# Last four stages of a hybrid model in one residency: the stream and its normalised form kept in SBUF from the fourth layer norm to the experts

## The reference, cut to what matters

```python
def _ln_t(v, eps=1e-5):
    m = jnp.mean(v, axis=-1, keepdims=True)
    s = jnp.var(v, axis=-1, keepdims=True)
    return (v - m) / jnp.sqrt(s + eps)
...
t = t + _L3_attn_ref(_ln_t(t), L3_attn_Wk, L3_attn_Wq, L3_attn_Wv)
t = t + _L3_ffn_ref(_ln_t(t), L3_ffn_router_w, L3_ffn_router_b, L3_ffn_expert_w, L3_ffn_expert_b)
```

## Time and profile before

| | before |
|---|---|
| median of three runs | 11067.49 us |
| the profiled execution | 11073.83 us, span 11072.0 us |
| TensorE busy | 10046.5 us, 91% of the span |
| VectorE busy | 6934.8 us, 63% |
| DRAM traffic of the queue of SyncE's DMAs | 1010.30 MB |
| ln4, from its first DMA issue to that of l3 | 10606.62 to 10664.38 us: 57.8 us |
| l3, to the first issue of ln5 | 10664.38 to 10770.31 us: 105.9 us |
| ln5, to the first issue of moe | 10770.31 to 10828.32 us: 58.0 us |
| moe, to the end | 10828.32 to 11072.0 us: 243.7 us |

### The profile page before, as it was taken

The page is one execution under the profiler, slowest core; times in us unless marked ns, Lnnn a source line. Parts: engine busy times, 40 slices in busy tenths (PEclk is TensorE's granted clock), DMA queues, the critical chain, the costliest instruction groups (busy, mean ns, idle before and its releaser), DMA issues. The chain is left out here.

```text
span 11072.0 us, 146129 instructions
## 1 busy us (share of the span) xinstructions
PE 10046.5 (91%) x45360; PEld 7803.1 (70%) x45360; DVE 6934.8 (63%) x8005; ACT 5276.4 (48%) x13704; POOL 5609.9 (51%) x2968
## 2 busy tenths in 40 slices
PE   7999999999967699999999689998599999999977
PEld 5677677667743588888888456565388887888854
DVE  6677677667755699999999644343533333333337
ACT  4787787778743677777777222222111111111110
POOL 4797788779743699999999126463100000000000
PEclk9999999999987799999999789999799999999988
DMA  2111111111124544444444510001745555455521
GB/s 81 26 39 40 38 30 38 41 26 39 32 88 163 189 107 108 105 108 108 105 105 108 195 56 8 14 10 73 254 123 130 128 128 159 127 133 123 125 105 64
DMA packets 646817, 1018.65 MB, mean 92 GB/s; under 512 B 285816, under 2 KB 347776, under 8 KB 631552
## 3 DMA queue, kind: packets, MB, share of 16 engines
q1 hardware_dynamic: 646176, 1010.30, 32.8%
HBM read 717.21 MB, written 211.03 MB: 84 GB/s over the span
## 5 line engine op out<-in xcount | busy, mean ns | idle before, releaser
L687 POOL TENSOR_TENSOR l_probs_low<-l_probs,l_probs_high 128x512 fp32r<-128x512 f32 x1792 | 2385.8, 1361 | 795.3 <-ACT l_probs_high L657 781.6
L1374 POOL TENSOR_TENSOR m_c_h<-m_h,m_c 128x2048 f32<-128x2048 f32 x520 | 2341.9, 4578 | 45.9 <-DVE m_h L1361 45.7
L1361 DVE TENSOR_TENSOR_SCAN m_h<-m_decay,m_ps_x 128x1024 f32<-128x1024 f32 x1040 | 2272.4, 2262 | 92.3 <-issue 64.5
L1274 PE MATMUL m_ps_y<-m_c_h,m_ident 128*128 128x256 f32 x8320 | 1981.6, 381 | 2.2 <-POOL m_c_h L1374 2.2
L743 DVE TENSOR_REDUCE l_max_by_row<-l_ps_all 128x8 f32<-128x512 f32 x2048 | 1358.0, 685 | 524.9 <-PE l_ps_all L506 444.4
L1274 PEld LDWEIGHTS m_ps_y<-m_c_h,m_ident 128*128 128x128 f32 x8320 | 1512.8, 191 | 174.1 <-POOL m_c_h L1374 4.9
L655 ACT ACTIVATE l_probs<-l_ps_all 128x512 f32<-128x512 f32 x2048 | 1240.4, 606 | 452.8 <-PE l_ps_all L547 307.0
L2350 PE MATMUL s_ps_all<-s_toeplitz,s_u_high 128*128 128x512 f32 (+1 forms) x4608 | 1327.9, 372 | 59.4 <-DMA s_toeplitz<-filters 50.3
L657 ACT ACTIVATE l_probs_high<-l_ps_all 128x512 fp32r<-128x512 f32 x2048 | 1233.0, 602 | 0.0
L2404 ACT ACTIVATE s_filtered_high<-s_rows 128x512 fp32r<-128x512 f32 x384 | 242.8, 632 | 1764.3 <-DVE s_rows L2477 898.4
L2350 PEld LDWEIGHTS s_ps_all<-s_toeplitz,s_u_high 128*128 128x128 f32 x4608 | 845.9, 189 | 240.0 <-DMA s_toeplitz<-filters 51.3
(11 more groups left out here) (320 smaller groups left out, 15384.1 us busy)
## 6 DMA issues: line engine op xcount, KB each, us to landing
m_delta_u<-du_t SPq DMA_DIRECT2D x1040, 128.0 KB, 3.7
s_toeplitz_sums<-filters SPq DMA_DIRECT2D x192, 642.0 KB, 6.7
s_toeplitz_sums<-filters SPq DMA_DIRECT2D x192, 386.0 KB, 5.7
m_c<-c_windows SPq DMA_DIRECT2D x130, 512.0 KB, 4.2
s_toeplitz<-filters SPq DMA_DIRECT2D x64, 770.0 KB, 9.3
s_toeplitz<-filters SPq DMA_DIRECT2D x64, 642.0 KB, 10.4
l_q_and_row_bias<-l_q_parts SPq DMA_DIRECT2D x64, 512.0 KB, 5.0
du_t<-m_delta_u_high SPq DMA_DIRECT2D x128, 256.0 KB, 3.1
```

The source lines that it names most:

```text
L687: pool.tensor_tensor(pl[:, slot, :], pt[:, slot, :], f(ph[:, slot, :]), ALU.subtract).then_inc(low_pool, 1)
L1274: ins = pe.matmul(y_ps[:, group % 2, 0:DIRS * SPAN].rearrange("p (d t) -> p d t", d=DIRS), ident[:, :], ch[:, group % CH, :, n, :], start= ...
L1361: dve.tensor_tensor_scan(h[:, u % H, :], decay[:, pair % 2, ct, k % 2, :, :].rearrange("p n t -> p (n t)"), x_ps[:, u % X, :], 0.0, ALU.mu ...
L1374: pool.tensor_tensor(ch[:, group % CH, 2 * pair % DIRS:2 * pair % DIRS + 2, :, :].rearrange("p d n t -> p d (n t)"), h[:, 2 * pair % H:2 * ...
```

## The change

The four stages get one common `Mem` in a new function `tail`. It holds the stream (`xs`), its normalised form (`xc`), and every weight but the experts' bias. `norm_kept` takes the place of `layer_norm`: the same arithmetic in the same order, but it reads the stream from the kept tile and leaves the normalised form in the other kept tile. The first of the two calls also loads the stream and nine weight tensors; the second issues no DMA. Neither stores anything. `linear_attention` and `experts` lose their loads (all but the experts' bias), their waits for them, and `linear_attention` its stores. Each of the four still opens its own `Mem` for its other tiles and semaphores, so the meeting of the engines between stages stays; `tail`'s own `Mem` adds one more closing block, with nothing to clear, at the very end.

```diff
+def norm_kept(nc, stage, xs, xc, cm, ident, eps, x=None, loads=()):
...
+        @block.sync
+        def _(sp):
+            if x is not None:
+                for dst, src in loads[:2]:
+                    sp.dma_start(dst[:], src).then_inc(weights, 16)
+                for q in range(LOTS):
+                    part = slice(q * LOT * TW, (q + 1) * LOT * TW)
+                    sp.dma_start(xs[:, part], x[:, part]).then_inc(loaded[q], 16)
+                for dst, src in loads[2:]:
+                    sp.dma_start(dst[:], src).then_inc(others, 16)
+                sp.wait_ge(others, 16 * (len(loads) - 2))
...
-def linear_attention(nc, stage, xn, x, x_out, wk_t, wq, wv_t, ident_in):
+def linear_attention(nc, stage, xs, res, ident, wks, wqs, wvs):
...
-        @block.sync
-        def _(sp):
-            for dst, src in ((ident, ident_in), (wks, wk_t), (wvs, wv_t), (wqs, wq), (xs, xn), (res, x)):
-                sp.dma_start(dst[:], src).then_inc(loaded, 16)
-            for b in range(BATCH):
-                sp.wait_ge(added, NTB * (b + 1))
-                sp.dma_start(x_out[:, b * L:(b + 1) * L], res[:, b * L:(b + 1) * L]).then_inc(stored, 16)
-            sp.wait_ge(stored, 16 * BATCH)
...
-            pe.wait_ge(loaded, 96)
...
-            dve.wait_ge(loaded, 96)
...
-def experts(nc, stage, xn, x, out, router_w, router_b, expert_w, expert_b, ident_in, rank_in):
+def experts(nc, stage, xs, res, out, ident, rw, rb, ew, rank, expert_b):
...
-            loads = ((ident, ident_in), (rw, router_w), (ew, expert_w), (rb, router_b),
-                     (rank, rank_in), (xs, xn), (res, x))
-            for dst, src in loads:
-                sp.dma_start(dst[:], src).then_inc(loaded, 16)
...
-            pe.wait_ge(loaded, 112)
...
-            dve.wait_ge(loaded, 112)
...
+def tail(nc, stage, x, out, a):
+
+    H, KQ, E = 8, 64, 8
+    with Mem(nc, stage) as keep:
+        xs, xc = keep.sb("x", [P, TOK]), keep.sb("xn", [P, TOK])
...
+        loads = ((cm, a["channel_mean"]), (ident, a["ident"]), (wks, a["wk_t"]), (wvs, a["wv_t"]), (wqs, a["wq_heads"]),
+                 (rw, a["router_w"]), (rb, a["router_b"]), (rank, a["rank8"]), (ew, a["expert_w"]))
+        norm_kept(nc, "ln4", xs, xc, cm, ident, 1e-5, x=x, loads=loads)
+        linear_attention(nc, "l3", xc, xs, ident, wks, wqs, wvs)
+        norm_kept(nc, "ln5", xs, xc, cm, ident, 1e-5)
+        experts(nc, "moe", xc, xs, out, ident, rw, rb, ew, rank, a["expert_b"])
...
-    xn4, x5, xn5 = act_map("xn4"), act_map("x5"), act_map("xn5")
-    layer_norm(nc, "ln4", x4, xn4, a["channel_mean"], a["ident"], 1e-5)
-    linear_attention(nc, "l3", xn4, x4, x5, a["wk_t"], a["wq_heads"], a["wv_t"], a["ident"])
-    layer_norm(nc, "ln5", x5, xn5, a["channel_mean"], a["ident"], 1e-5)
-    experts(nc, "moe", xn5, x5, out, a["router_w"], a["router_b"], a["expert_w"], a["expert_b"], a["ident"], a["rank8"])
+    tail(nc, "tail", x4, out, a)
```

More of the change, by code:

```diff
@@ L2503, in _, with at, take_variance, spread_out @@
             add(PASSES - 1, 7)
-def linear_attention(nc, stage, xn, x, x_out, wk_t, wq, wv_t, ident_in):
+def norm_kept(nc, stage, xs, xc, cm, ident, eps, x=None, loads=()):
+    LOT = 4
+    LOTS, COLS = NT // LOT, LOT * TW // P
+    with Mem(nc, stage) as m:
+        sq = m.sb("square", [P, TOK])
+        epst = m.sb("eps", [P, 1])
+        std, rstd = m.sb("deviation", [P, LOTS, COLS]), m.sb("reciprocal", [P, LOTS, COLS])
+        mean_ps, var_ps, wide_ps = m.ps("mean", [P, 2, TW]), m.ps("variance", [P, 2, TW]), m.ps("reciprocal", [P, 2, TW])
+        weights, own, loaded = m.sem("weights"), m.sem("own"), [m.sem(f"loaded{q}") for q in range(LOTS)]
+        mean, centred, squared, variance, deviation, recip, spread, normed, others = (
+            m.sem(n) for n in ("mean", "centred", "squared", "variance", "deviation", "recip", "spread", "normed", "others"))
+        block = m.block()
+        def at(t):
+            return slice(t * TW, (t + 1) * TW)
+        @block.sync
[9 more added lines that the diff above has]
+                sp.wait_ge(others, 16 * (len(loads) - 2))
+        @block.tensor
+        def _(pe):
+            if x is not None:
+                pe.wait_ge(weights, 32)
+            def take_variance(t):
+                q, k = t // LOT, t % LOT
+                pe.wait_ge(squared, t + 1)
+                if k == 0 and q >= 2:
+                    pe.wait_ge(deviation, q - 1)
+                for n in range(TW // P):
+                    col = k * (TW // P) + n
+                    ins = pe.matmul(var_ps[:, q % 2, col:col + 1], sq[:, t * TW + n * P:t * TW + (n + 1) * P], cm[:, 0:1], start=True, stop=True)
+                ins.then_inc(variance, 1)
+            def spread_out(t):
+                q, k = t // LOT, t % LOT
+                pe.wait_ge(recip, q + 1)
+                if t >= 2:
+                    pe.wait_ge(normed, t - 1)
+                for n in range(TW // P):
+                    col = k * (TW // P) + n
+                    ins = pe.matmul(wide_ps[:, t % 2, n * P:(n + 1) * P], rstd[:, q, col:col + 1].to_broadcast((P, P)), ident[:, :], start=True, stop=True)
+                ins.then_inc(spread, 1)
+            for t in range(NT):
+                if t % LOT == 0 and x is not None:
+                    pe.wait_ge(loaded[t // LOT], 16)
+                if t >= 2:
+                    pe.wait_ge(centred, t - 1)
+                pe.matmul(mean_ps[:, t % 2, :], cm[:, :], xs[:, at(t)], start=True, stop=True).then_inc(mean, 1)
+                if t >= 1:
+                    take_variance(t - 1)
+                if t >= LOT + 2:
+                    spread_out(t - LOT - 2)
+            take_variance(NT - 1)
+            for t in range(NT - LOT - 2, NT):
+                spread_out(t)
+        @block.scalar
+        def _(act):
+            act.wait_ge(own, 1)
+            for t in range(NT):
+                q = t // LOT
+                act.wait_ge(centred, t + 1)
+                act.activation(sq[:, at(t)], xc[:, at(t)], ACT.Square).then_inc(squared, 1)
+                if t % LOT == LOT - 1:
+                    act.wait_ge(variance, t + 1)
+                    act.activation(std[:, q, :], var_ps[:, q % 2, 0:COLS], ACT.Sqrt, bias=epst[:, :]).then_inc(deviation, 1)
+        @block.vector
+        def _(dve):
+            dve.memset(epst[:, :], eps).then_inc(own, 1)
+            def normalise(t):
+                dve.wait_ge(spread, t + 1)
+                dve.tensor_tensor(xc[:, at(t)], xc[:, at(t)], wide_ps[:, t % 2, :], ALU.mult).then_inc(normed, 1)
+            def invert(q):
+                dve.wait_ge(deviation, q + 1)
+                dve.reciprocal(rstd[:, q, :], std[:, q, :]).then_inc(recip, 1)
+            for t in range(NT):
+                dve.wait_ge(mean, t + 1)
+                if t % LOT == 0 and x is not None:
+                    dve.wait_ge(loaded[t // LOT], 16)
+                dve.tensor_tensor(xc[:, at(t)], xs[:, at(t)], mean_ps[:, t % 2, :], ALU.subtract).then_inc(centred, 1)
+                if t % LOT == 1 and t > LOT:
+                    invert(t // LOT - 1)
+                if t >= LOT + 2:
+                    dve.wait_ge(squared, t - LOT - 1)
+                    normalise(t - LOT - 2)
+            invert(LOTS - 1)
+            for t in range(NT - LOT - 2, NT):
+                dve.wait_ge(squared, t + 1)
+                normalise(t)
@@ L2520, in linear_attention @@
         mix_ps = m.ps("mix", [P, TW])
-        loaded, turned, copied, grammed = (m.sem(n) for n in ("loaded", "turned", "copied", "grammed"))
+        turned, copied, grammed = (m.sem(n) for n in ("turned", "copied", "grammed"))
         gram_ok, kg_done, kg_ok, ktv_done, ktv_ok, mixed, mix_ok = (
             m.sem(n) for n in ("gram_ok", "kg_done", "kg_ok", "ktv_done", "ktv_ok", "mixed", "mix_ok"))
-        outed, added, stored = m.sem("outed"), m.sem("added"), m.sem("stored")
+        outed, added = m.sem("outed"), m.sem("added")
         block = m.block()
-        @block.sync
-        def _(sp):
-            for dst, src in ((ident, ident_in), (wks, wk_t), (wvs, wv_t), (wqs, wq), (xs, xn), (res, x)):
-                sp.dma_start(dst[:], src).then_inc(loaded, 16)
-            for b in range(BATCH):
-                sp.wait_ge(added, NTB * (b + 1))
-                sp.dma_start(x_out[:, b * L:(b + 1) * L], res[:, b * L:(b + 1) * L]).then_inc(stored, 16)
-            sp.wait_ge(stored, 16 * BATCH)
         @block.tensor
         def _(pe):
-            pe.wait_ge(loaded, 96)
             for b in range(BATCH):
@@ L2617, in experts @@
         xt_ps = m.ps("x_by_token", [P, 2, TW])
-        loaded, own = m.sem("loaded"), m.sem("own")
+        own = m.sem("own")
         logits, gated, shifted, expd, mixed, turned, accd, turned_ok = (
```

10 lines of the change are left out of this document (4 added, 6 removed).

## The result

Five runs of the changed kernel against five of the kernel before: median 10996.56 us (10976.72 to 11021.98) against 11067.49 us (11065.08 to 11083.72); ratio 0.9934, 95% interval 0.9918 to 0.9950. The forecast was 10989 us, a ratio of 0.9929. The profiled execution took 10996.56 us with a span of 10994.8 us.

A forecast was written before the change was run, and what follows sets the result against it. At three seams, 77.62 us together, DMA alone was on the path; elsewhere the compute engines set the pace. 73.1 + 1.9 + 1.5 + 2.4 - 0.5 = 78.4 us off 11067.5 gave 10989 us, range 10975 to 11003.

The forecast's parts named there:

- three terms of 30.86, 12.25 and 30.01 us: Time removed at seams ln4/l3, l3/ln5 and ln5/moe, leaving 1.5 us at each; together 73.1 us.
- The added loads: Seven more weight loads in ln4, 1.55 MB, 4.5 us of transfer, hidden behind the stream's parts; taken as nothing.
- Rival 3: In ln4 the added weight loads delay the stream by 4.5 us: 73.9 us saved, 10993.6 us; chance 0.05.
- sum of three terms less the closing block: Clock gains at stage starts, 1.9 us in l3, 1.5 in ln5, 2.4 in moe, less 0.5 for tail's closing block.
- an idle time of 2.3 us: TensorE's pause at a seam, claimed just short enough that each following stage starts at 2.4 GHz.
- 2.5 us of logits at double pace: At moe's start the logits run at the full clock for 2.5 us before it falls, winning 2.4 us.
- Rival 1: In moe the logits hold the full clock, winning 13.8 us instead of 2.4: 10977.7 us; chance 0.09.
- Rival 2: Stage starts cost more than 1.5 us and the clock gains are lost: 66.9 us saved, 11000.6 us; chance 0.09.
- rival 5: At the seams another engine is late by as much, so nothing is gained: about 11067 us; chance 0.02.
- rival 4: moe's expert loop slows as VectorE's tiles lie elsewhere; 0.122 us per instruction would cancel the gain; chance 0.01.

The follow-up runs named there:

- e8: Changed kernel with the router's logits moved into ln5 and three extra wide products in ln2, ln3 and ln4; median 10980.07 us, ratio 0.9923 to the kernel before.
- e7: Changed kernel with three extra 512-column products in ln2, ln3 and ln4 while TensorE would wait for the load; median 10985.90 us.
- e9: Changed kernel with 20 extra 512-column products in moe's logits, four in front and one ahead of every four logits products; moe took 223.8 us.
- e3: Changed kernel with the seven further weight loads issued ahead of the stream's four parts in ln4; tail 403.9 us, 17.3 more than the changed kernel.

## Why the prediction was right

**The seams.** The three terms of 30.86, 12.25 and 30.01 us came out as 30.99, 12.54 and 30.15. Taking 1.5 us for what is left was one to three tenths too much: 1.37, 1.21 and 1.36. The construction of a seam from a store's landing, a meeting, a clearing and a load was tested by putting one part back, and gave 5.43 and 7.67 us where 5.3 and 7.7 were to be expected. Nothing that the load wait had covered appeared in TensorE's first steps: its first product starts 0.1 us behind its release. By the rule that spoke against it (the Trainium skill, "Runtime: NRT & Kernel Launch", section "Instruction fetch mechanics") a taken branch costs a fetch if its target is not in the engine's instruction memory. No seam here, 1.21 to 1.37 us long, shows a fetch; whether the targets were in that memory no run shows.

**The added loads.** Taken at nothing, because they are last in the queue: ln4 became 0.13 us longer and its start 0.27 us shorter. Ahead of the stream they cost 5.5 us. Rival 3 had about the right price (4.5) for the wrong order.

**The clock.** The sum of three terms less the closing block was 5.3 us, and l3, ln5 and moe won 4.98. One by one they were less good, and the reading under them was wrong. TensorE's last work before the seams ln5/moe (kernel before) and ln4/l3 (changed kernel):

```profile
10818.09 4.09 PE L209 MATMUL ln_ps_reciprocal<-ln_ident,ln_reciprocal 128*128 128x128 f32 x32 [0.40 <-DVE ln_centred L243]
10657.68 2.02 PE L2559 MATMUL ln_ps_reciprocal<-tail_ident,ln_reciprocal 128*128 128x128 f32 x16
```

The first ends at 10822.18, and the clock fell 0.9 us into the stretch from 10824, at 10824.9: 2.7 us later, not 3.7. So the two falls that the prediction read came 2.7 to 2.8 us behind the last work, and an idle time of 2.3 us had half a microsecond to spare, not one and a half.

- ln5: 1.56 for 1.5. TensorE idled 1.94 us, and no fall came. In the kernel before, the clock fell 5.0 us behind l3's last product (10761.92 to 10766.9), later than behind the norms.
- l3: the step that failed is that 2.3 us of idling is short enough. TensorE idled 2.17 us; the clock fell at about 10662.65, 3.0 us behind the last work and 0.8 us after l3's first product, so the cold start stayed. l3 won 3.26 us all the same, because in the first image's small products, where the clock had dropped to 0.61, it held (1.00 from 10684 to 10687). I had taken the inside of l3 for unchanged, so 3.26 for 1.9 is not this term coming true.
- moe: the logits took 26.31 us instead of 27.49, 1.2 us won for 2.4. The clock fell where the prediction put it, 3.4 us behind ln5's last product. But the engine idles 2.2 us of that, which my 2.5 us of logits at double pace left out: 1.3 us of them are left (0.79 in the stretch 10777 to 10780). The rest of the stage took 1.0 us more, 0.3 of it tail's closing block (taken as 0.5); where the other 0.7 went I only infer: the clock rose 4.4 us behind the first product after the gates and 3.0 before.

**Rival 1**, the logits at the full clock, is out: 0.50 throughout but for the start. The sentence in the Trainium skill's "TensorE: Matmul & The Clock Gate", section "What's actually happening", that activity releases the throttle, can't be read as busy time here: 23.00 us of unbroken work in the logits left the clock at 0.50. Rival 2 is out by the seams, none over 1.37 us, though l3's clock was lost as it says; rival 5 by both intervals, which lie below 1; and rival 4 by the expert loop: 508 and 641 instructions with 154.62 and 164.89 us busy before and 155.32 and 164.70 after, in its last 172 us and its last 172.8:

```profile
10822.00:10994.80 172.80, 155.32 (x508) 82.24 (x508) 164.70 (x641) 0.00 (x0) 0.00 (x0) 0.98 0.09 25
```

**The total.** Between profiles the tail gives 78.9 us. Between medians it was 70.9 and 59.5 us in the two larger comparisons; over all 12 runs of the changed kernel and 18 of the kernel before, the medians are 10994.8 and 11067.5, 72.6 us apart. That is as near to rival 2's 66.9 as to the forecast's 78.4: the total could not have told them apart, the seams did. The four profiled executions of the changed kernel average 10991.8 us and the eight others 11002.1. What those eight have that the four haven't is not in any trace and stays open; a norm that stays at the lower clock costs 8 to 14 us, the right size, and a slow m3 as in e8 some 18 us, but both are argued, not shown.

## What to carry to other kernels

Where stages hand a tensor through DRAM with a barrier between them, the price of a seam is read from four rows, the store's landing, the meeting, the clearing and the load, and keeping the tensor in SBUF gives back all but about 1.3 us of it; the weights alone gave a seventh. Loads that nobody needs yet are free behind the urgent ones and not ahead of them. And a pause costs more than its length if the work behind it is a mixture that does not raise TensorE's clock: wide products put first raised it in e7, e8 and e9, though the mixture behind them lost it again once (e8).

## What the runs showed of the hardware that was not expected

- TensorE, busy 24.79 of 25 us, stayed at 1.2 GHz (e3), and the same mixture of two records of 512 columns to eight of 8 or 1 ran at 2.4 GHz for 22 us once dense products had raised the clock (e9).
- In the four profiles of the changed kernel the clock fell 2.8 to 3.0 us behind the last work of ln4, although TensorE had idled only 2.2 us and was at work again; behind l3, with 1.9 us of idling, it did not fall.
- A layer norm that starts behind a load so has two lengths, 57.3 to 58.4 or 65.5 to 71.7 us, with no change in its code; it goes with the mean clock, 0.93 against 0.73 to 0.78 where it was read.
- Three wide products ahead of it, some 5.4 us in a wait that was there anyway, gave 56.5 to 57.0 us for ln2 and ln3 in all four cases seen, though ln4 lost its clock once even so.
- Four small DMAs and 1.1 MB ahead of 8 MB cost 5.1 us, not the 3.2 us of their bytes.
